# A second attention whose maximum enters as 16 extra rows of the score product, with 8 KB loads in three buffers

## The reference, cut to what matters

```python
q = (h @ wq).reshape(B, S, N_HEADS, D_HEAD)
k = (h @ wk).reshape(B, S, N_HEADS, D_HEAD)
v = (h @ wv).reshape(B, S, N_HEADS, D_HEAD)
scores = jnp.einsum('bhsd,bthd->bhst', q, k) * scale
attn = jax.nn.softmax(scores, axis=-1)
ctx = jnp.einsum('bhst,bthd->bshd', attn, v).reshape(B, S, d)
```

## Time and profile before

| | us |
|---|---|
| median of 3 runs | 915.25 (914.11 to 917.23) |
| the profiled execution | 919.9 |
| its span on the core | 917.8 |

### The profile page before, as it was taken

How to read it: one execution, slowest core, us unless ns; L and a number is a source line. 1 busy time by engine, 2 the same in 40 slices (tenths; PEclk the granted TensorE clock), 3 DMA queues, 4 the chain that set the end, 5 groups by cost and what they waited for, 6 DMA issues and landing times. The chain is left out here.

```text
span 917.8 us, 19246 instructions
## 1 busy us (share of the span) xinstructions
PE 811.5 (88%) x7380; PEld 547.7 (60%) x7381; DVE 464.6 (51%) x1079; ACT 337.1 (37%) x568; POOL 148.4 (16%) x155
## 2 busy tenths in 40 slices
PE   4899999999988996999998878875989999999994
PEld 2466666666667874666666764542556666666662
DVE  7666665655536553667664773610124444444441
ACT  5566666666623443455543222200111111111110
POOL 4000000000003341000000220174002222222222
PEclk7599999999979997999998897987999999999997
DMA  5200000000011565699981600023012222222221
GB/s 199 94 2 2 2 2 2 2 2 2 4 41 35 135 129 114 89 181 172 163 176 53 217 1 14 12 107 125 24 34 46 46 46 46 46 46 46 46 40 18
DMA packets 68493, 58.88 MB, mean 64 GB/s; under 512 B 5504, under 2 KB 60104, under 8 KB 68432
## 3 DMA queue, kind: packets, MB, share of 16 engines
q1 hardware_dynamic: 60512, 47.60, 23.1%
q0 software_dynamic: 7152, 9.38, 6.2%
q10 hardware_dynamic: 768, 1.02, 0.4%
HBM read 35.02 MB, written 22.95 MB: 63 GB/s over the span
## 5 line engine op out<-in xcount | busy, mean ns | idle before, releaser
L1124 DVE TENSOR_REDUCE fa_m<-ps 128x2 bf16<-128x512 f32 x128 | 81.7, 684 | 35.1 <-PE ps L1022 34.4
L1365 POOL DMA_INDIRECT out<-ex_Y,ex_to x39 | 60.6, 1554 | 215.9 <-DVE ex_Y L1615 212.8
L1104 ACT ACTIVATE fa_PT<-ps 128x1024 f32<-128x1024 f32 x64 | 65.6, 1024 | 68.2 <-PE ps L1040 68.2
L624 ACT ACTIVATE la_PT<-ps 128x512 f32<-128x512 f32 x128 | 69.5, 594 | 33.4 <-PE ps L530 33.4
L1433 PE MATMUL ps<-WG,ex_xT 128*128 x156 | 74.4, 600 | 0.6 <-ACT ex_xT L1493 0.6
L1446 PE MATMUL ps<-WD,ex_hT 128*128 x312 | 73.9, 380 | 0.9 <-DVE ex_hT L1599 0.9
L1433 PE MATMUL ps<-WU,ex_xT 128*128 x156 | 74.2, 598 | 0.0
L1495 ACT ACTIVATE ex_sl<-ps 128x512 f32<-128x512 f32 x39 | 23.3, 597 | 135.1 <-PE ps L1433 135.1
L657 DVE TENSOR_REDUCE la_m<-ps 128x4 bf16<-128x512 bf16 x64 | 44.3, 692 | 48.6 <-PE ps L523 47.6
L1595 DVE TENSOR_TENSOR ex_hd<-ps,ex_sl 128x512 f32<-128x512 f32 x39 | 27.0, 692 | 80.2 <-PE ps L1433 80.2
L638 DVE CAST V<-ps 96x512 bf16<-96x512 f32 x64 | 44.0, 687 | 38.0 <-PE ps L495 38.0
(11 more groups left out here) (255 smaller groups left out, 1417.1 us busy)
## 6 DMA issues: line engine op xcount, KB each, us to landing
QK<-qk_parts SPq DMA_DIRECT2D x96, 128.0 KB, 5.0
qk_parts<-pj_parts SPq DMA_DIRECT2D x16, 384.0 KB, 2.7
expert_in<-zfill SPq DMA_DIRECT2D x1, 5070.0 KB, 16.1
ex_XR<-expert_in SPq DMA_DIRECT2D x39, 130.0 KB
WG<-in_e_gate SPq DMA_DIRECT2D x8, 512.0 KB, 9.0
WU<-in_e_up SPq DMA_DIRECT2D x8, 512.0 KB, 9.6
WD<-in_e_down SPq DMA_DIRECT2D x8, 512.0 KB, 8.9
out<-HS SPq DMA_DIRECT2D x4, 512.0 KB, 3.1
```

What stands on the lines that cost most here:

```text
L624: nc.scalar.activation(PT[:, n % 2, jh], ps[:, 2 * (n % 2) + jh], ACT.Exp, scale=QK_SCALE).then_inc(s_exp[jh], 1)
L1104: nc.scalar.activation(PT[:, grp % 2, k:k + 2], ps[:, 2 + 2 * (hp % 2):4 + 2 * (hp % 2)].rearrange("p k (j i) -> p k j i", j=2), ACT.Exp, ...
L1124: nc.vector.reduce_max(m[:, par, h], ps[:, h % 2].rearrange("p (f j) -> p f j", f=2), AX.X).then_inc(s_max, 1)
L1365: nc.gpsimd.indirect_dma_start(out=outs, out_offset=bass.IndirectOffsetOnAxis(ap=to[:, n:n + 1], axis=0), in_=Y[:, n], in_offset=None, com ...
```

## The change

- The maximum is subtracted inside the score product. `QK` gets 16 more rows. On the key side they hold, written once for each buffer, which of a half batch's eight heads a row belongs to (`select`, from `hsel`). On the query side they hold minus the maxima. For each half batch TensorE transposes the maxima of eight heads (`turn_max`), ScalarE copies the 16 x 128 result to SBUF (`keep_max`), and GpSimd writes it to the rows in two instructions, each masked to one half of the queries (`rows`). The matmuls of line 1040 are gone, and `less_max` is four matmuls over 112 rows.
- The scores for the maximum run eight pairs of heads, one batch, ahead of `less_max`; `weigh` is cut in two halves, one a pair. The loops are written out.
- The copy of the sums goes from VectorE to ScalarE (`keep_out`), the copy of the values from ScalarE to GpSimd (`values`).
- `qk_parts` is laid out by batch, with channels ordered so that a row of `QK` is one run of 8 KB. A batch is 6 loads: for each group of 3, 2 and 1 slots, one for the left side and one for the right side, in which one block of 16 rows is read 3, 2 or 1 times. There are three buffers; batches 0 to 2 are loaded in `project`.
- `WU` is loaded in `route` beside `WD`; only `WG` stays in `full_attention`.

```diff
-LEFT = (0, 0, 1, 0, 2, 1)
-RIGHT = (0, 1, 0, 2, 0, 1)
+LEFT = (0, 1, 2, 0, 1, 0)
+RIGHT = (0, 0, 0, 1, 1, 2)
...
+RB = 3
+HR = 16
+KR = KP + HR
...
-        g.qd = nc.dram_tensor("qk_parts", [2, 3, D, T], BF16, kind="Internal").ap()
+        g.qd = nc.dram_tensor("qk_parts", [2, B, 3, D, S], BF16, kind="Internal").ap()
...
-                g.QK = upper.enter_context(nc.sbuf_tensor("QK", [KP, 2, 2, H, S], BF16))
+                g.QK = upper.enter_context(nc.sbuf_tensor("QK", [KR, RB, 2, H, S], BF16))
...
-                g.WG, g.WU = kept_right("WG", [P, E, DC, F]), kept_right("WU", [P, E, DC, F])
+                g.WG = kept_right("WG", [P, E, DC, F])
                 full_attention(nc, g, a)
-            g.WD = kept_right("WD", [P, E, FC, D])
+            g.WU, g.WD = kept_right("WU", [P, E, DC, F]), kept_right("WD", [P, E, FC, D])
...
-                        sp.dma_start(qd[k, :, :, t * GC:(t + 1) * GC], parts[:, t % 2, k].rearrange("p a (m t) -> p (a m) t", m=DC)
+                        sp.dma_start(qd[k, :, t:t + 1], parts[:, t % 2, k].rearrange("p a (m t) -> p (a m) t", m=DC).unsqueeze(1)
                                      ).then_inc(s_st[t % 2], 16)
 
                 for t in range(GN):
                     if t >= 2:
                         b, part = divmod(t - 2, 3)
                         sp.wait_ge(s_st[b], 32)
-                        load_packed(g, sp, b, b, range(2 * part, 2 * part + 2))
+                        load_packed(g, sp, b, (part,))
+                sp.wait_ge(s_st[0], 64)
+                load_packed(g, sp, 2)
...
-def load_packed(g, sp, b, par, slots=range(SLOTS)):
-    src = g.qd.rearrange("k a (h d) t -> k a d h t", d=DK)
-    for k, side in enumerate((LEFT, RIGHT)):
-        for n in slots:
-            sp.dma_start(g.QK[n * DK:(n + 1) * DK, par, k], src[k, side[n], :, :, bass.ds(b * S, S)]).then_inc(g.s_ld[par], 16)
+GROUPS = ((0, 3), (3, 2), (5, 1))
+def load_packed(g, sp, b, groups=(0, 1, 2)):
+    for at, n in (GROUPS[x] for x in groups):
+        to = slice(at * DK, (at + n) * DK)
+        sp.dma_start(g.QK[to, b % RB, 0], g.qd[0, b, 0:n].rearrange("a (d h) t -> (a d) h t", h=H)).then_inc(g.s_ld[b % RB], 16)
+        same = g.qd[1, b, RIGHT[at]:RIGHT[at] + 1].rearrange("a (d h) t -> a d (h t)", h=H).to_broadcast([n, DK, H * S])
+        sp.dma_start(g.QK[to, b % RB, 1], same).then_inc(g.s_ld[b % RB], 16)
 def full_attention(nc, g, a):
...
+    (s_sc, s_max, s_mt, s_mtc, s_row, s_lg, s_exp, s_pv, s_ot, s_vs, s_pad) = (
+        sem("fa_" + n) for n in "scores max turned kept rows less exp pv out values pad".split())
+    PAIRS = B * HP
+    HALF = HP // 2
+    HH = H // 2
+    LEAD = HP
+    LOADED = 2 * len(GROUPS) * 16
+    AT = slice(KP, KR)
         m = sb("m", [P, 2, H, 2], BF16)
+        MT = sb("MT", [P, 2, P], BF16)
         PT = sb("PT", [P, 2, 4, 2, S], F32)
         Vs = sb("Vs", [P, 2, 2, H, PADV], F32)
+        rmask, hsel = sb("rmask", [P, 2], F32), sb("hsel", [P, H], F32)
+        MX = ps[0:HR, 7].bitcast(BF16)[:, 0:P]
             @block.sync
             def _(sp):
...
+                sp.dma_start(rmask[:], a["rmask"]).then_inc(g.s_zd, 16)
+                sp.dma_start(hsel[:], a["hsel"]).then_inc(g.s_zd, 16)
+                for b in range(RB, B):
+                    sp.wait_ge(s_lg, (b - RB + 1) * HP)
+                    load_packed(g, sp, b)
+                    for e in range((b - RB) * E // (B - RB), (b - RB + 1) * E // (B - RB)):
+                        sp.dma_start(g.WG[:, e], a["e_gate"][e].rearrange("(c p) f -> p c f", p=P)).then_inc(g.s_w, 16)
             @block.tensor
             def _(pe):
...
+                def scores(x):
+                    b, h = divmod(x, H)
+                    if h == 0:
+                        pe.wait_ge(s_ld[b % RB], (b // RB + 1) * LOADED)
+                    if x >= 2:
+                        pe.wait_ge(s_max, x - 1)
                     for half in range(2):
...
+                        last = mm(ps[:, h % 2, half * S:(half + 1) * S], QK[0:KP, b % RB, 0, h, half * P:(half + 1) * P], QK[0:KP, b % RB, 1, h],
                                   start=True, stop=True)
                     last.then_inc(s_sc, 1)
...
+                def turn_max(q):
+                    b, hh = divmod(q, 2)
+                    pe.wait_ge(s_max, (q + 1) * HH)
+                    if q:
+                        pe.wait_ge(s_mtc, q)
+                    nc.tensor.transpose(MX, m[:, b % 2, hh * HH:(hh + 1) * HH].rearrange("p h f -> p (h f)"), g.identB[:]).then_inc(s_mt, 1)
+                def less_max(x):
+                    b, hp = divmod(x, HP)
+                    if hp == 0 and b < RB:
+                        pe.wait_ge(s_pad, b + 3)
+                    if x % HALF == 0:
+                        pe.wait_ge(s_row, 2 * (x // HALF + 1))
+                    if x >= 2:
+                        pe.wait_ge(s_exp, x - 1)
                     for k in range(2):
                         h = 2 * hp + k
...
                         for jh in range(2):
...
+                            last = mm(ps[:, 2 + 2 * (x % 2) + k, jh * S:(jh + 1) * S], QK[:, b % RB, 1, h, jh * P:(jh + 1) * P], QK[:, b % RB, 0, h],
+                                      start=True, stop=True)
                     last.then_inc(s_lg, 1)
...
+                def weigh(y, jhs):
+                    b, grp = divmod(y, NG)
+                    if jhs[0] == 0:
+                        if grp == 0:
+                            pe.wait_ge(s_vs, b + 1)
+                        pe.wait_ge(s_exp, 2 * y + 2)
+                        if y % 2 == 0 and y:
+                            pe.wait_ge(s_ot, y // 2)
+                    for jh in jhs:
                         for k in range(4):
...
+                            last = mm(ps[32 * k:32 * k + PADV, 6, (y % 2) * S:(y % 2 + 1) * S],
+                                      Vs[:, b % 2, jh, 4 * grp + k], PT[:, y % 2, k, jh], start=jh == 0, stop=jh == 1, skip_group_check=True)
+                    if jhs[-1] == 1:
+                        last.then_inc(s_pv, 1)
+                for x in range(2 * LEAD):
+                    scores(x)
+                    if x == HH + 1:
+                        turn_max(0)
+                for x in range(PAIRS):
+                    ahead = 2 * (x + LEAD)
+                    if ahead < B * H:
+                        scores(ahead)
+                    less_max(x)
+                    if ahead < B * H:
+                        scores(ahead + 1)
+                    if x % HALF == 0 and x // HALF + 1 < 2 * B:
+                        turn_max(x // HALF + 1)
+                    if x >= 2:
+                        weigh(x // 2 - 1, (x % 2,))
+                weigh(PAIRS // 2 - 1, (0, 1))
             @block.gpsimd
             def _(pool):
...
+                def select(r):
+                    do(G.tensor_copy(QK[AT, r, 1], hsel[AT].unsqueeze(2).to_broadcast([HR, H, S])))
+                def values(b):
+                    if b >= 2:
+                        pool.wait_ge(s_pv, (b - 1) * NG)
+                    G.tensor_copy(Vs[:, b % 2, :, :, 0:DK], g.V2[:, 2 * b:2 * b + 2]).then_inc(s_vs, 1)
+                    pool.wait_ge(s_vs, b + 1)
+                def rows(q):
+                    b, hh = divmod(q, 2)
+                    pool.wait_ge(s_mtc, q + 1)
+                    for half in range(2):
+                        G.tensor_scalar(QK[AT, b % RB, 0, hh * HH:(hh + 1) * HH, half * P:(half + 1) * P],
+                                        MT[AT, q % 2].unsqueeze(1).to_broadcast([HR, HH, P]), rmask[AT, half:half + 1], None, ALU.mult).then_inc(s_row, 1)
+                        pool.wait_ge(s_row, 2 * q + half + 1)
+                pool.wait_ge(g.s_zd, 48)
+                select(0)
+                do(G.memset(Vs[:, :, :, :, DK:PADV], 0.0))
+                do(G.memset(Vs[:, :, :, :, DK:DK + 1], 1.0))
+                values(0)
+                rows(0)
+                rows(1)
+                for b in range(1, B):
+                    if b < RB:
+                        select(b)
+                    rows(2 * b)
+                    values(b)
+                    rows(2 * b + 1)
             @block.scalar
             def _(act):
...
+                def keep_max(q):
+                    act.wait_ge(s_mt, q + 1)
+                    if q >= 2:
+                        act.wait_ge(s_row, 2 * (q - 1))
+                    nc.scalar.activation(MT[AT, q % 2], MX, ACT.Copy).then_inc(s_mtc, 1)
+                def keep_out(z):
+                    b, two = divmod(z, 2)
+                    act.wait_ge(s_pv, 2 * z + 2)
+                    nc.scalar.activation(g.OT[:, 2 * b:2 * b + 2, 2 * two:2 * two + 2], ps[:, 6].rearrange("p (g f i) -> p f g i", g=2, f=2),
+                                         ACT.Copy).then_inc(s_ot, 1)
+                keep_max(0)
+                for x in range(PAIRS):
+                    act.wait_ge(s_lg, x + 1)
+                    y = x // 2
```

(20 more changed lines are left out.)

## The result

The changed kernel takes 947.22 us (median of 4 runs, 945.12 to 949.22) where the kernel before takes 915.85 on the same chip: ratio 1.034, 95% interval 1.031 to 1.037, so 3.4% slower. The forecast was 912.9 us and its range ended at 927. The profiled run took 947.28 us with a span of 945.4. The experiments ran on three other chips, on each of which the kernel before takes 893 us, so they are compared by their ratio to it; the changed kernel was run on one of them too (c_after).

The account below looks back on a forecast made before the run. TensorE's own list was taken as the bound: first `less_max` 381.2, clock 3.5, pairs 86.8, stalls 12.0, last pairs 8.4, tail 0.65 and 3.2 gave 495.8 against 498.15, so 912.9 us, range 886 to 927.

Parts of the forecast that it names:

- TensorE's pace: Second attention's steady state: 1.45 to 1.65 us a pair of heads, taken as 1.55, against 2.19 before.
- The masked multiply: GpSimd's row instruction on 1024 elements: priced as a copy at 1.1 us, at most 2.3 as the two-input subtraction.
- The formula around it: GpSimd's rows per half batch: 2.2 us for exponential and `keep_max`, then two instructions, against 6.2 for four pairs.
- The rival: GpSimd's row instructions take 2.3 us or more: 917 to 920 us, more from 2.7 us upwards; chance 0.06.
- The cut at the outermost dimension: Right-side loads repeating a block 3 or 2 times use only 3 or 2 DMA engines, one carrying 312 KB.
- Engine 0 at 25.0 GB/s: The most loaded DMA engine moves its part of a packed batch at 25.0 GB/s, 12.8 us a batch.
- 12.0 of stalls: TensorE waits for packed loads 2.4 us before each of five batches, 14.9 us a load against 12.4.
- 3.5 of clock: TensorE's clock falls while idle before the first `less_max` and takes 7 us to rise: half, 3.5 us, lost.
- the slower rival: Engine 0 at 22.1 GB/s: fill ends 2.5 us later, stalls 4.2 us each, 924.4 us; chance 0.22 with what lies between.
- The fill: Stage start to first `less_max`: `rmask` and `hsel` land at 373, GpSimd's chain takes 8.2 us, first `less_max` at 381.2.
- `WU` hidden in the routing: Loading `WU` in `route`, 4.2 MB or 12 us at 353 GB/s, costs nothing; at most 12 us without cover.
- The sum: Second attention's terms together: stage ends at 495.8 against 498.15, 2.35 us less, 912.9 us on the median.

Follow-up runs that it names:

- c_after: The changed kernel run again unaltered on one of the experiments' chips: ratio 1.038 to the kernel before.
- e3_both: Changed kernel with right sides loaded as six DMAs of 16 rows and maxima masked before GpSimd spreads them: ratio 0.983 to the kernel before.
- m_forms: Changed kernel with GpSimd building the rows in four ways (mask column, constant, two tensors, copy then mask column): 934.66 us, a single execution.
- e1_spread: Changed kernel with each batch's right sides loaded as six DMAs of 16 rows instead of three repeating ones: ratio 1.018 to the kernel before.
- e2_copy: Changed kernel with GpSimd masking the 16 x 128 maxima first, then spreading them by plain copies: ratio 1.027 to the kernel before.
- e5_stripe: e3_both plus mask and select tables loaded early, each slot and side one 16-row DMA onto every sixth partition: ratio 0.980 to the kernel before.

## Why the prediction was wrong, step by step

- *TensorE's pace, 1.55 us a pair*: right, 1.55. Line 1040's 28 us are gone, as e3_both's body of 101.9 us shows. VectorE and ScalarE hide behind TensorE, as said.
- *The masked multiply, 1.1 us, at most 2.3*: wrong, and this is the first step that failed. It measured 2.84. I chose the copy's row "since it has one tensor input", and took the two-input row for an upper bound; m_forms shows that the form costs more than either, and the two-tensor one 1.89. The formula around it was right: 2.2 + 2 x 2.84 = 7.9 us for a half batch, measured 7.96, against four pairs' 6.2. The rival had its place and its chance of 0.06, but "917 to 920, and more from 2.7 us upwards" gave no price beyond. Alone it costs 29.3 us of body (e1_spread against e3_both).
- *The cut at the outermost dimension*: right; shares of 0.12 to 0.20 are left behind each load, where e1_spread goes from 0.96 to 0.02 within 4 us (403 to 409).
- *Engine 0 at 25.0 GB/s, 12.8 us for a batch*: wrong. The few engines do run at 25 GB/s, but the left sides and the weights go first, over all 16 engines, and there an engine makes 10 to 12. The "few engines compete then" of the prediction was the false step, and so was 353 GB/s as the rate of all engines, from rows that wrote weights to 128 partitions. A load took some 20 us (issued at 399.14 and awaited until 419.11 for batch 3), not 12.8. Alone this costs 34.9 us of body (e2_copy against e3_both), where the forecast had 12.0 of stalls and 3.5 of clock, and the slower rival 9 more. (By that rival's own numbers a stall is 14.5 + 2.3 - 12.4 = 4.4 us and not 4.2, so it should have read some 925 us.)
- *The fill*: `hsel` landed at 373.9 (forecast 373), the first `less_max` came at 385.45 (381.2): the 4.3 us are the two multiplies, 5.8 instead of 2.2, and small things.
- *`WU` hidden in the routing*: right.
- *The sum*: the stage ended 33.2 us later than forecast: 4.3 before the first `less_max` and 29 behind it. From the first exponential the changed kernel needs 40 us more than e3_both, and that had been priced at 15.5. Both errors went the same way, and they don't add: together 39.6 us of body where each alone has 29.3 and 34.9. The rest lies in the forecast's base: from the first `less_max` to the next stage it had 99 us without stalls and clock, and e3_both, with a little of both, takes 103. A range from the two rivals one at a time would still have missed. The right price for the multiply alone wouldn't have been enough either. With 2.84 us in it the same sum gives some 932 us, an estimate: 14 half batches at 7.96 us instead of 6.2 add 24.6, the last two 3.2 and the fill 3.5, and the stalls of 12.0 go, since 14.9 us for a load then lie below the 15.9 of a batch. e1_spread, whose loads are out of the way, measured 932 on this scale, and the 15 us from there to 947 are the load's.

What stays open: by what mechanism 16 engines that write adjacent partitions are slowed down, and why GpSimd's one-tensor form is dearer than its two-tensor form. The runs show that it is so, not why.

## What to carry to other kernels

Price an instruction on an engine by its own form: a row of another form, even one with more inputs, is no upper bound, and where none of the form is in the trace, the range has to hold the case in which its chain passes the pace. Rate a load by the partitions it lands on and by everything that is queued with it on its slowest engine, not by the best rate of any transfer. When two limits lie in parallel, undoing one shows little; undo both before you call either harmless, and compare stretches of the stage, since totals mix in where the stage starts.

## What the runs showed of the hardware

- GpSimd, 16 x 1024 bf16: copy 1.04 us, multiply of two tensors 1.89, multiply of one tensor by a column or a constant 2.84 and 2.77; for 128 elements a row the last form took 0.60.
- Packed loads with a third of weights among them, rate by the busy share of the engines: 16 rows of 8 KB on adjacent partitions 156 GB/s, on every sixth partition 307, 512-byte runs on adjacent partitions 120. Weights alone, on 128 partitions, made 360 in the changed kernel. SyncE's 14 issues of such loads took 7.1, 9.1 and 10.6 us in the same order.
- TensorE's granted clock over the stage was 0.80 with the stops and 0.92 in e5_stripe, over the body 0.86 and 0.98; behind the stop of 10.15 us, at a granted clock of 0.50 (1.2 GHz), four matmuls took 1.06 us instead of 0.61, so a stop costs more than its own length.
